# Moving the copy of the V product between two exponentials in a distance-attention stage

## The reference

```python
x = layernorm(x)
qh, kh, vh = heads(x @ Wq), heads(x @ Wk), heads(x @ Wv)      # 16 heads of 8
dist = maximum(sum(qh*qh) - 2 * qh @ kh.T + sum(kh*kh).T, 0)
scores = exp(-gamma * D**-0.5 * dist)
scores = where(triu(ones, k=1), scores, 0)                     # only later keys
out = (scores @ vh) @ Wo
```

## Time and profile before

| what | value |
|---|---|
| median of 3 runs | 1855.53 us (1855.27 to 1855.6) |
| profiled execution, first to last instruction | 1853.5 us |
| outside the span, by the median | 2.0 us |
| distance stage | the first 456 us |
| mean granted TensorE clock | 0.970 of full speed |

### The profile page before, as it was taken

One profiled execution on the slowest core, in us unless ns is written; L12 is line 12 of the kernel. 1 busy time (PEld: TensorE's weight loads), 2 busy tenths in 40 slices (PEclk: granted clock), 3 DMA queues, 4 the chain that ended last, 5 costly groups with the idle time before them and its releaser, 6 DMA issues. The chain is left out here.

```text
span 1853.5 us, 67967 instructions
## 1 busy us (share of the span) xinstructions
PE 1676.8 (90%) x27513; PEld 1287.6 (69%) x27513; DVE 1449.6 (78%) x3461; ACT 1437.3 (78%) x4100; POOL 753.0 (41%) x842
## 2 busy tenths in 40 slices
PE   3888898886899999999997996879999999999797
PEld 1444444443688888888886774658888888888686
DVE  8999999998677678877887766747777777789674
ACT  4989999996788888888774666658888888877464
POOL 2010000000255444455446866425454545455694
PEclk7999999998999999999999997989999999999999
DMA  6565556551001010101012000000101010001211
GB/s 194 140 155 146 149 124 148 132 149 28 13 15 25 14 26 14 26 14 26 14 26 48 2 2 1 1 12 15 25 14 26 15 25 18 22 14 25 48 47 47
DMA packets 80040, 91.95 MB, mean 50 GB/s; under 512 B 11696, under 2 KB 67984, under 8 KB 79728
## 3 DMA queue, kind: packets, MB, share of 16 engines
q1 hardware_dynamic: 78432, 87.15, 19.0%
q10 hardware_dynamic: 1296, 0.44, 0.1%
HBM read 39.68 MB, written 31.10 MB: 38 GB/s over the span
## 5 line engine op out<-in xcount | busy, mean ns | idle before, releaser
L1519 POOL TENSOR_TENSOR f1l_pn<-f1l_p,f1l_rs 128x512 f32<-128x512 f32 (+1 forms) x256 | 207.9, 834 | 259.3 <-DVE f1l_rs L1206 258.2
L1519 POOL TENSOR_TENSOR f2l_pn<-f2l_p,f2l_rs 128x512 f32<-128x512 f32 (+1 forms) x256 | 207.9, 834 | 248.8 <-DVE f2l_rs L1206 248.7
L1078 ACT ACTIVATE f2l_p<-f2l_sm,f2l_nb 128x192 f32<-128x192 f32 x512 | 214.7, 444 | 43.9 <-DVE f2l_nb L1199 43.9
L1078 ACT ACTIVATE f1l_p<-f1l_sm,f1l_nb 128x192 f32<-128x192 f32 x512 | 214.8, 444 | 42.0 <-DVE f1l_nb L1199 42.0
L417 PE MATMUL r_acc<-r_pr,r_vp 128*32 128x128 f32 (+2 forms) x3584 | 197.9, 338 | 6.9 <-DVE r_pr L630 6.0
L527 ACT ACTIVATE r_pr<-r_far 128x1536 f32<-128x1536 f32 x128 | 195.4, 1526 | 3.3 <-PE r_far L401 3.0
L622 DVE SCALAR_TENSOR_TENSOR r_pr<-r_pr,k_lo,r_cap 128x512 f32<-128x512 f32 x256 | 180.7, 746 | 11.0 <-ACT r_pr L527 10.9
L630 DVE TENSOR_SCALAR r_pr<-r_pr,k_hi,k_lo 128x768 f32<-128x768 f32 x256 | 164.5, 684 | 0.0
L527 ACT ACTIVATE r_pr<-r_near 128x1024 f32<-128x1024 f32 x128 | 139.6, 1091 | 1.1 <-PE r_near L388 1.1
L1524 POOL MEMSET k_rtz<- 128x132 f32 x1 | 0.2, 208 | 337.3 <-POOLq L688 337.3
L417 PEld LDWEIGHTS r_acc<-r_pr,r_vp 128*32 128x32 f32 x3584 | 89.1, 112 | 49.7 <-issue 31.2
(11 more groups left out here) (505 smaller groups left out, 5158.7 us busy)
## 6 DMA issues: line engine op xcount, KB each, us to landing
rbf_rows<-r_part SPq DMA_DIRECT2D x112, 128.0 KB, 2.3
r_qs<-rbf_rows SPq DMA_DIRECT2D x60, 192.0 KB
r_ks<-rbf_rows SPq DMA_DIRECT2D x60, 192.0 KB
f1l_vs<-f1l_vv SPq DMA_DIRECT2D x64, 128.0 KB, 2.4
f2l_vs<-f2l_vv SPq DMA_DIRECT2D x64, 128.0 KB, 2.4
rbf_rows<-r_part SPq DMA_DIRECT2D x16, 384.0 KB, 3.1
rbf_rows<-r_part SPq DMA_DIRECT2D x16, 256.0 KB, 3.2
out<-k_x SPq DMA_DIRECT2D x8, 512.0 KB, 3.2
```

The source lines that it names most:

```text
L1078: ins = nc.scalar.activation(p[:, u % 2, k, :], sm[:, u % 2, k // 2, k % 2 * PW:(k % 2 + 1) * PW], ACT.Exp, bias=nb[:, u % 2, k:k + 1], ac ...
L1519: ins = nc.gpsimd.tensor_tensor(pn[:, u % 2, at:at + HU * w].rearrange("p (k c) -> p k c", k=HU), p[:, u % 2, :, cols], r.broadcast_to([P, ...
```

## The change

In the distance stage ScalarE's copy of the V product (k = USES - 1, made ahead at pair 3) no longer follows the far exponential of pair 3. It stands one pair later, after the near and before the far exponential of pair 4. The other products are taken out where they were. TensorE, VectorE, GpSimd and the DMA queues have the same programs as before.

```diff
                     exps(n, slice(0, ON), near[:], s_dg, s_exd)
+                    if w and ahead(b, w - 1) and ahead(b, w - 1)[1] == USES - 1:
+                        leave(*ahead(b, w - 1))
                     exps(n, slice(ON, RCOLS), far[:, :, 0:RCOLS - ON], s_of, s_exo)
                     if w == 2 and b:
                         leave_values(b - 1)
                     if split(b, w):
                         second_part(*split(b, w))
-                    if ahead(b, w):
+                    if ahead(b, w) and ahead(b, w)[1] < USES - 1:
                         leave(*ahead(b, w))
```

## The result

| | median us | range us |
|---|---|---|
| before, beside these runs | 1855.4 | 1853.95 to 1855.6 (4 runs) |
| changed | 1864.43 | 1862.95 to 1870.45 (4 runs) |
| changed, measured again (e1) | 1863.61 | 1861.77 to 1864.7 (5 runs) |
| before, beside e1 | 1852.31 | 1848.49 to 1855.83 (17 runs) |

The ratio is 1.0076 (95% interval 1.0061 to 1.0092) in the first comparison and 1.0062 (1.0049 to 1.0076) in the second, so 9 to 11 us slower. The forecast was 1870 in 1859 to 1874. One run of e5 (2315 us) and one of e8 (6014 us) were slow ones and are in no median, range or ratio.

What follows compares the result with a forecast made beforehand. ScalarE, with VectorE nearly as tight, was taken to bound the distance stage. Added wait of 5.9 us plus 8.8 for repeating half-clock stretches gave 14.7, so 1855.5 became 1870.2 us, range 1859 to 1874.

Steps and rivals of the forecast that it cites:

- The replaced wait: ScalarE, pairs 3 and 4: 0.52 us wait becomes about 0.9 for near scores; 0.39 per batch, 5.9 us in all.
- VectorE: At pair 4: masking may start 0.10 us earlier, bounding 0.39 later; nothing later in the batch gives it back.
- The output projection: On TensorE, waiting for the moved copy: delayed by under 0.1 us, on an engine with room.
- The clock: TensorE half-clock stretches at pair 3: once one hits, every following batch is hit and lasts 27.3 us; 8.8 us.
- The count: Disturbed batches in the distance stage: 9 to 14 instead of 6, taken as 12.
- the lower bound of 9.7 us: Distance stage: total loss with 9 disturbed batches, 3.8 us for the clock together with 5.9 for the wait.
- Batch 3 dropping out: Its stretch comes early by 0.6 to 0.8 us, may drop out in batch 4, caught again about batch 9.
- A: The forecast itself: added wait plus repeating half-clock stretches in the distance stage, 1864 to 1873.5 us; chance 0.60.
- B: Rival: added wait alone, five to seven half-clock stretches as before, 1859.5 to 1863 us; chance 0.20.
- C: Rival: faster or nothing lost, as shifted batches make stretches miss the V product's chain; 1852.2 with all gone; chance 0.10.
- D: Rival: VectorE is the bound, the earlier near exponential gains up to 1.5 us, 1854 us; chance 0.05.
- E: Rival: all 14 stretches, and later stages that lose more, above 1873.5 us; chance 0.05.

Runs made afterwards that it cites:

- e5: Kernel before, with an added ScalarE copy of 128x128 constants behind the V product's copy in batches 0 to 14: 1854.25 us (1.0015).
- e8: Kernel before, with TensorE making the V product and pair 4's near scores before the second portion of value matmuls: 1850.95 us (1.0002).
- e9: Changed kernel, with TensorE making the V product and pair 4's near scores before the second portion of value matmuls: 1852.29 us (0.9994).
- e4: Kernel before, with an added ScalarE copy of 128x384 constants behind the V product's copy in batches 0 to 14: 1871.32 us (1.0109).
- e6: Kernel before, with an added ScalarE copy of 128x768 constants behind the V product's copy: 1863.56 us (1.0059).
- e2: Kernel before, with two unused matmuls (768 columns in all) in TensorE's gap ahead of pair 3's far scores: 1853.07 us (1.0005).
- e3: Changed kernel, with two unused matmuls (768 columns in all) in TensorE's gap ahead of pair 3's far scores: 1861.01 us (1.005).
- e7: Kernel before, with one unused matmul of 384 columns in TensorE's gap ahead of pair 3's far scores: 1852.91 us (1.0009).
- e10: e9 with one unused matmul of 384 columns in TensorE's gap ahead of pair 3's far scores: 1850.57 us (0.999).
- e12: e10, with TensorE at pair 4 also making the far scores before the first portion of value matmuls: 1851.24 us (1.0007).
- e11: Changed kernel, with the V product's copy one place further, behind pair 4's far exponential, TensorE as before: 1870.81 us (1.0093).

## Why the prediction was right, and where it was off

**The replaced wait.** Forecast 0.52 + 0.39 = 0.91 before the near exponential; measured 0.91. Forecast 0.39 (bounds 0.33 and 0.39) per batch; measured 0.37 to 0.39 (25.77 against 25.40; 26.12 against 25.73 with the filler). The sum of 5.9 is 5.6 to 5.9. Taking the release of a near exponential by its own scores from the earlier trace rows gave the better bound. e9 shows the cause: with the scores early the same moved copy costs nothing beside e8.

**VectorE.** Right: masking follows without idle time, bounding waits 0.42. That neither engine gives the time back holds too. The output projection was sized too small: counted from pair 3's far scores it starts after 5.21 us instead of 5.01 (at 208.41 in the batch above), so 0.20 later and not under 0.1; ScalarE does not wait for the near scores behind it.

**The clock.** The mechanism was right, though not from the start of the stage on. A disturbed batch that would last 27.2 to 27.4 settles at 27.3, and the stretch then hits every batch (the changed kernel twice, e4 from batch 2 on). e4 shows it without the change; e6 had one stretch without a repetition, e5 none to repeat. That the stretches depend on TensorE's gap ahead of pair 3's far scores rests on counts: in batches 1 to 14 the five traces with the gap filled (e2, e3, e7, e10, e12) have none, the nine without a filler have 13, 9, 6, 6, 6, 3, 1, 1 and, in e5, none. As e5 shows, one trace without a stretch would prove little; five out of five make it likely. All stretches of the nine in these batches but one (e11, batch 4, 6.7 us after the far scores) began within 1.1 us of pair 3's far scores.

**The count, the term that was mis-sized.** I took 12 disturbed batches, of 9 to 14; the two profiles have 6 and 9. With six, as before, the term for the clock, forecast at 8.8 us, is nothing: the stage is 7.5 us longer and the profiled span 9.1. The error was to let the run start in batch 1 as the likelier case: the trace of before had one start of the stretches, and I took it for the start of every run, since three runs agreed within 0.33 us. They do not agree: 17 later runs of the same kernel spread over 7.3 us, and e1 and the first profile differ in batches 1 to 3. That was an inference from three numbers and it was wrong; the lower bound of 9.7 us was the better forecast. The base was uncertain too: the six stretches of the kernel before come from one profile, of a run at about 1855.5 us, and the later medians of 1850.3 to 1852.3 suggest that most of its runs have fewer. Batch 3 dropping out and the catch at batch 9 (e1) came as described.

**Luck in the number.** The prediction named six stretches again as a sign that it was wrong, and the first profile has exactly six. What puts 1864.4 inside A's range all the same are 5.6 us of wait, 1.9 in batches 0 to 2 and 1.6 in the later stages; no term had forecast the last two. e1's median of 1863.6 lies just below A's 1864, over a base that was 3 us lower. In e1, with nine stretches, the sum for the stage does come out by the forecast's own terms.

**The rivals.** B (wait alone, 1859.5 to 1863) was nearly as good in time as A, since the first profile has as many stretches as before; what separates them is the unbroken run, and it is there. C and D are refuted: the stretches did not get fewer than before (six and nine), and VectorE gained nothing. Of E nothing was seen: the slowest of nine runs took 1870.45 us.

**Left open.** Why e4 was caught at batch 2, and its runs were all above 1871, while the unbroken run in both profiles of the changed kernel began at batch 9; the two are about equally late per batch. And why the later stages take 1404.4 to 1406.6 us in the three traces with the small filler (e7, e10, e12), when the two with the large one have 1399.5 and 1399.6 and the nine without 1397 to 1400.5; no run tells the filler from chance there. In e7 and e10 it is not the clock: their later stages have 60 and 65 us at half clock, the kernel before 65. e12 was built to beat both kernels; its stage is the shortest, its time is not.

## What to carry to other kernels

Before moving work out of a wait, ask what the wait is hiding: here the copy that seemed to stand in the way covered the time in which the next scores were made, and moving it only replaced a 0.52 us wait by one of 0.91. With the scores made early (e9) the move cost nothing; but it gained nothing either, as the engine then waited elsewhere. In this loop, where a disturbed batch of 27.2 to 27.4 us met stretches of half clock 27.3 us apart, a lateness of 5.9 us in all cost 19 us, and one of 10.6 us cost 12. So read from the trace how far apart such stretches are before making a loop a little longer.

## What the runs showed of the hardware

TensorE's granted clock went from 2.4 to 1.2 GHz for 3.4 us at a time, and successive stretches began 27.3 us apart (e1, e4). The loss was not monotonic in the lateness: 0.18, 0.39 and 0.71 us per batch cost 3, 19 and 12 us, the 3 not clear of nothing (1.0015, 0.9998 to 1.0033). In e11 the same locking appears over two batches: from batch 7 on, disturbed batches of 28.06 to 28.16 us alternate with undisturbed ones of 26.57, together 54.6 to 54.7, twice 27.3. The granted clock fell to its lower level after TensorE had stood idle for only 0.94 us at a time, as the earlier trace rows show; with the gap filled it was not seen to fall there. The Trainium skill (TensorE: Matmul & The Clock Gate, section HAM oscillation — how this bites in real kernels) describes a clock that falls once per loop turn because of long waits on DMAs; the repetition per turn is what the traces show here, but with short waits on another engine. And the time of one kernel varied with nothing changed, over 7 us in 17 runs beside e1 and over 10 us in 23 beside e9, so that three runs within 0.33 us had said little.
